# One penalty tile per step, an earlier last batch, and one activation table for exponential and logarithm in a decoder layer

## What is computed

```python
g = sigmoid(x @ Wg + bg)
res = (1 - Z_I) * maximum(1 - Z_I - Z_J, 0) + Z_I * minimum(1 - Z_I + Z_J, 1)   # Z_I = g, Z_J = g transposed
scope = clip(power(s - 2, 1 - g) + 2 - abs_ij, 1e-32, 1.0)
log_pen = log(maximum(res * scope, 1e-32))
scores = q @ k.T / sqrt(16) + log_pen          # 16 heads of 16
x = layernorm(x + softmax(scores) @ v)
x = layernorm(x + cross_attention(x, ctx, mask) @ Wo + bo)
x = layernorm(x + quantised_ffn(x))
```

## Time and profile before

| | us |
|---|---|
| median of 3 runs (lowest, highest) | 772.19 (771.64, 775.09) |
| the profiled execution, its own time | 774.11 |
| its span in the trace | 772.3 |
| PE busy | 659.1 (85%) |
| DVE busy | 591.6 (77%) |
| ACT busy | 489.1 (63%) |
| POOL busy | 327.6 (42%) |

### The profile page before, as it was taken

The page is one execution under the profiler, slowest core; times in us unless marked ns, Lnnn a source line. Parts: engine busy times, 40 slices in busy tenths (PEclk is TensorE's granted clock), DMA queues, the critical chain, the costliest instruction groups (busy, mean ns, idle before and its releaser), DMA issues.

```text
span 772.3 us, 10412 instructions
## 1 busy us (share of the span) xinstructions
PE 659.1 (85%) x3348; PEld 264.2 (34%) x3350; DVE 591.6 (77%) x1299; ACT 489.1 (63%) x809; POOL 327.6 (42%) x417
## 2 busy tenths in 40 slices
PE   6478879999899899998799899998889899984952
PEld 3232224434223243343233343443223235233331
DVE  3988984686899866676997766569986796827986
ACT  4435566556557968654568787554587576773964
POOL 6316766566754414645653135546603110101503
PEclk9778999999999999999999999999999899997977
DMA  2832352320423324313205213342321520000003
GB/s 95 193 93 72 96 135 64 91 60 25 98 60 85 85 44 112 85 44 71 71 24 134 57 52 93 69 109 64 88 65 44 128 59 3 4 3 0 1 0 109
DMA packets 35749, 53.84 MB, mean 70 GB/s; under 512 B 5232, under 2 KB 26736, under 8 KB 35696
## 3 DMA queue, kind: packets, MB, share of 16 engines
q1 hardware_dynamic: 35696, 53.18, 26.5%
HBM read 36.91 MB, written 14.68 MB: 67 GB/s over the span
## 4 chain that ended last, share of the span: by engine, by line
PE 44%; DVE 27%; POOL 11%; ACT 8%; issue 7%; DMA 2%; SPq 0%; POOLq 0%; DVEq 0%; ACTq 0%
PE ps L1583 10%; POOL probs L733 8%; PE ps L1559 8%; PE ps L1536 7%; DVE dist L1026 5%; PE ps L1420 5%; PE ps L1523 5%; DVE mx L1023 4%; ACT probs L918 4%; PE ps L1516 3%; DVE pen_a L1089 2%; DVE pen_a L1085 1%; PE ps L1564 1%; PE ps L1563 1%; DVE pen_a L1093 1%
## 5 line engine op out<-in xcount | busy, mean ns | idle before, releaser
L1536 PE MATMUL ps<-KS,QS 96*128 96x512 bf16 x512 | 201.0, 395 | 36.1 <-DVE mx L1026 13.2
L918 ACT ACTIVATE probs<-ps 128x512 f32<-128x512 f32 x256 | 148.9, 596 | 127.3 <-PE ps L1564 92.3
L733 POOL TENSOR_TENSOR probs<-probs,penT 128x512 f32<-128x512 f32 x128 | 168.5, 1336 | 109.8 <-ACT probs L918 109.8
L1023 DVE TENSOR_REDUCE mx<-ps 128x1 f32<-128x512 f32 x256 | 169.0, 684 | 54.9 <-PE ps L1536 54.3
L1559 PE MATMUL ps<-QS,KS 108*128 108x512 bf16 x512 | 196.6, 386 | 12.9 <-ACT probs L918 9.1
L918 ACT ACTIVATE probs<-ps,mask_col 128x512 f32<-128x512 f32 x256 | 166.6, 689 | 47.1 <-PE ps L1559 45.0
L1026 DVE CUSTOM_DVE_ANT_0 dist<-ps,mask_rest 128x512 bf16<-128x512 f32 x192 | 126.3, 684 | 26.4 <-PE ps L1536 26.1
L1536 PEld LDWEIGHTS ps<-KS,QS 96*128 96x128 bf16 x512 | 50.7, 99 | 186.4 <-DVE mx L1026 64.8
L1559 PEld LDWEIGHTS ps<-QS,KS 108*128 108x128 bf16 x512 | 50.1, 99 | 90.0 <-ACT probs L918 55.1
L1583 PE MATMUL ps<-probs,v_s 128*32 128x512 f32 x512 | 68.2, 604 | 14.3 <-POOL probs L733 14.3
L1583 PE MATMUL ps<-probs,v_c 128*32 128x512 f32 x512 | 69.1, 612 | 0.9 <-ACT probs L918 0.9
(11 more groups left out here) (195 smaller groups left out, 939.5 us busy)
## 6 DMA issues: line engine op xcount, KB each, us to landing
parts_qs<-parts SPq DMA_DIRECT2D x8, 384.0 KB, 2.6
parts_ks<-parts SPq DMA_DIRECT2D x8, 384.0 KB, 2.8
KS<-parts_ks SPq DMA_DIRECT2D x16, 192.0 KB, 3.6
QS<-parts_qs SPq DMA_DIRECT2D x16, 192.0 KB, 4.0
parts_kc<-parts SPq DMA_DIRECT2D x8, 384.0 KB, 2.9
KS<-parts_kc SPq DMA_DIRECT2D x16, 192.0 KB, 3.1
...
```

The lines of the kernel that those rows point to most:

```text
L733: g.tensor_tensor(probs[:, T % NP, :], probs[:, T % NP, :], penT[:, MUL_KT.index(kt), :], ALU.mult)\
L918: s_.activation(probs[:, T % NP, :], ps[:, exp_bank(T), :], ACT.Exp, bias=bias)\
L1023: v.tensor_reduce(mx[:, n % 2, t, j:j + 1], ps[:, MAX_BANKS[(TG * n + i) % AHEAD], :], AX.X, ALU.max)\
L1536: mm(ps[:, MAX_BANKS[(TG * n + i) % AHEAD], :], QS[0:SK, slot, j, t * P:(t + 1) * P], KS[0:SK, slot, j, :], start=True, stop=True).then_in ...
```

## The change

Three things change, all of them in the plan but for one line of ACT.

1. The penalty tiles of batches 1, 2 and 3 are dealt out one to a step, where s02, c00, c01 and c10 had two: batch 1 in s01, s02, s03, s10; batch 2 in s13, c00, c01 and, with seven hand-set slots, c02 and c03; batch 3 in s22, s23, c10, c11. The gate of batch 2 moves from s13 to s12, the fetch of x^T for it from s12 to s10. The logarithm of batch 1 moves from slot 14 of s03 to slot 15 of s10, that of batch 2 from slot 0 of c03 to its slot 15; batch 3's stays.
2. For the last batch the residual, its norm and the two query projections start four to six slots earlier: the residual in slots 1 to 4 of c22 instead of 7 to 10, the norm in 6 to 10 instead of 13 to 15, the first projection in slot 13 of c22 and the second in slot 1 of c23, instead of slots 1 and 5 of c23.
3. ACT loads the table set `natural_log_exp_and_others` at the very start, and the exponential of one column there goes.

```diff
     if what in ("q", "k"):
-        jobs = [(what, *rest, c) for c in range(HC)]
+        jobs = [task] if len(rest) == 3 else [(what, *rest, c) for c in range(HC)]
...
-    add(("s", 0, 2), stacks=[], fetch=[("queries", 0), ("xres", 0)], tasks=[(1, 11, ("k", "s", 1)), (0, 15, ("pens", 1, (1, 2)))])
-    add(("s", 0, 3), at=[(14, ("ln", 1))], fetch=[("mask", 0), ("xres", 1)], tasks=[(0, 13, ("pens", 1, (3,)))])
-    add(("s", 1, 0), fetch=[("masks", 1)], tasks=[(1, 11, ("k", "c", 0)), (8, 14, ("v", "c", 0))])
+    add(("s", 0, 2), stacks=[], fetch=[("queries", 0), ("xres", 0)], tasks=[(1, 11, ("k", "s", 1)), (0, 15, ("pens", 1, (1,)))])
+    add(("s", 0, 3), fetch=[("mask", 0), ("xres", 1)], tasks=[(0, 13, ("pens", 1, (2,)))])
+    add(("s", 1, 0), at=[(15, ("ln", 1))], fetch=[("masks", 1), ("xT", 2)],
+        tasks=[(1, 11, ("k", "c", 0)), (8, 14, ("v", "c", 0)), (0, 11, ("pens", 1, (3,)))])
...
-    add(("s", 1, 2), at=[(1, ("v", "s", 1, 1))], fetch=[("xT", 2)], tasks=[(1, 5, ("residual", 0)), (8, 12, ("ln1", 0))])
-    add(("s", 1, 3), at=[(15, ("mask_col",))], tasks=[(1, 6, ("q", "c", 0)), (7, 8, ("mask", 0)), (3, 14, ("gate", 2))])
-    add(("c", 0, 0), fetch=[("cT", 1)], tasks=[(0, 15, ("pens", 2, (0, 1)))])
-    add(("c", 0, 1), tasks=[(2, 13, ("q", "s", 2)), (0, 15, ("pens", 2, (2, 3)))])
-    add(("c", 0, 2), tasks=[(0, 10, ("k", "s", 2)), (8, 15, ("residual", 1))])
-    add(("c", 0, 3), at=[(0, ("ln", 2))], tasks=[(5, 14, ("v", "s", 2)), (15, 15, ("mask", 1)), (0, 0, ("x1bias", 0)), (2, 13, ("ln1", 1))])
+    add(("s", 1, 2), at=[(1, ("v", "s", 1, 1))], tasks=[(1, 5, ("residual", 0)), (8, 12, ("ln1", 0)), (3, 13, ("gate", 2))])
+    add(("s", 1, 3), at=[(15, ("mask_col",))], tasks=[(1, 6, ("q", "c", 0)), (7, 8, ("mask", 0)), (2, 13, ("pens", 2, (0,)))])
+    last_tile = expand(("pens", 2, (3,)))
+    add(("c", 0, 0), fetch=[("cT", 1)], tasks=[(0, 15, ("pens", 2, (1,)))])
+    add(("c", 0, 1), tasks=[(2, 13, ("q", "s", 2)), (0, 15, ("pens", 2, (2,)))])
+    add(("c", 0, 2), at=[(3 * k, job) for k, job in enumerate(last_tile[:3])],
+        tasks=[(0, 10, ("k", "s", 2)), (8, 15, ("residual", 1))])
+    add(("c", 0, 3), at=[(3 * k, job) for k, job in enumerate(last_tile[3:])] + [(15, ("ln", 2))], tasks=[(5, 14, ("v", "s", 2)), (15, 15, ("mask", 1)), (0, 0, ("x1bias", 0)), (2, 13, ("ln1", 1))])
...
-        add(("s", b, 3), fetch=[("cT", b)] + ([] if more else [("weights", 0)]), tasks=[(0, 9, ("wo", b - 2)), (12, 15, ("ln2", b - 2))])
+        add(("s", b, 3), fetch=[("cT", b)] + ([] if more else [("weights", 0)]), tasks=[(0, 9, ("wo", b - 2)), (12, 15, ("ln2", b - 2))]
+            + ([(0, 13, ("pens", b + 1, (1,)))] if more else []))
...
-            add(("c", b - 1, 0), fetch=[("xres", b)], tasks=[(0, 15, ("pens", b + 1, (1, 2)))])
+            add(("c", b - 1, 0), fetch=[("xres", b)], tasks=[(0, 15, ("pens", b + 1, (2,)))])
...
-            add(("c", b - 1, 2), tasks=[(7, 10, ("residual", b)), (13, 15, ("ln1", b))])
-            add(("c", b - 1, 3), tasks=[(0, 4, ("q", "c", b)), (14, 14, ("x1bias", b))])
+            add(("c", b - 1, 2), tasks=[(1, 4, ("residual", b)), (6, 10, ("ln1", b)), (13, 13, ("q", "c", b, 0))])
+            add(("c", b - 1, 3), tasks=[(1, 1, ("q", "c", b, 1)), (14, 14, ("x1bias", b))])
...
-            act.wait_ge(consts, 1)
-            s_.activation(table_call[:, 0:1], ones_f[:, 0:1], ACT.Exp)
+            s_.preload_act_table_set("natural_log_exp_and_others")
```

## The result

The changed kernel takes 767.5 us, the median of seven runs, beside 773.51 us of the kernel before on the same chip. Six of the seven lie between 763.41 and 768.6 us, and one, at a granted clock of 0.65, took 941.61 us and is left out of the ratio. That is 0.9906, 95% interval 0.9882 to 0.9931. Repeated, it was 0.9930 (0.9905 to 0.9955). So it is faster by 0.7 to 0.9%, some 5 to 7 us, where 20.7 us (to 751.5, range 744 to 763) was forecast: right in sign, a third of the size or less, and outside the range.

The account below looks back on a forecast made before the run. No engine bounds the whole: DVE binds s02, c00, c01 and c10, PE binds s10, s13 and s23. Terms -13.3, -1.5, +0.5, +0.9 - 3.0, +1.5, -2.3, -3.5 sum to -20.7 us: 772.2 to 751.5, range 744 to 763.

Parts of the forecast that it names:

- part 1: One penalty tile per step: s02 -2.5, c00 -4.0, c01 -3.5, c10 -3.3 us, together -13.3.
- The tables' part: Eight table loads go; gains on the path of s10 -1.5, c03 -3.0 and c13 -2.3 us.
- rival 1: Relieved steps meet PE waits DVE hid, give half; s10 gains nothing, s23 loses 3.0; -11.0 us, 761.2; chance 0.20.
- The cost of a tile, (22.5 - 11.4)/15: In s02, DVE's time beyond its maxima over 15 penalty operations: 0.74 us each, 5.2 us per tile of seven.
- c01 by the pattern of c11, 17.8: c01 with one tile was to take 17.8 us like c11, which has the same query projection: -3.5 us.
- s10 (-1.5): Table loads give 2.6 us less about 1.1; the added tile is hidden under PE's 21.6 us.
- s12 and s13 (+0.5): Batch 2's gate moves to s12 (+3.0 us); s13 loses it and takes a tile (-2.5 us).
- c02 and c03 (-2.1): Shared tile 3 of batch 2 costs +0.9 us; table loads and half clock gone from c03 give -3.0.
- c13 (-2.3), s23 (+1.5): c13 loses two table loads, 2.6 us less 0.3; s23 takes a tile, 0 to +5.2 us.
- rival 3: Each of six table loads on the path also costs a drain, 1.28 us: 7.7 us more, 743.8; chance 0.03.
- The last batch (-3.5): c22, c23 and c30: PE's 2.4 us query-stack wait and a third of 3 us of clock go; range 0 to -7.
- Rival 2: mT is late at slot 8 of c23 and the clock halves behind it: 3.5 us lost, 755.0; chance 0.12.

Follow-up runs that it names:

- the tables alone: Kernel before with only the first exponential replaced by one table-set load: 0.9873, and 0.9914 on another chip.
- short products: Changed kernel with POOL's multiplications of probabilities by penalties cut from 512 to 64 columns: 732.83 us in one execution.
- the product a slot later: Context product of multiplied tiles one slot later on PE, in kernels with table load and mT first: 0.9834, repeated 0.9857, with old tile places; 0.9800 with moved.
- the second trace: Changed kernel run again with nothing altered, against the kernel before: 0.9930.
- mT first: Kernel before with table load and last batch moved, shift row mT sent between c30's key and query loads, tiles in old places: 0.9901.

## Why the prediction was wrong, point by point

**The step that failed.** It is part 1: -13.3 us for four relieved steps, and -10.4 for the moved tiles as a whole. Alone they gave nothing (1.0002, 0.9986 to 1.0018). By PE's starts and against the tables alone the four relieved steps give 5.5 us, and s12, c03, s23, s10 and s11, less s13, take some 6.3, for which 2.9 was booked. Two things were wrong in it, the next bound and the price of a tile. The tables' part came out as forecast (6.2 of 6.8 us).

**The reading of the four steps as bound by DVE: half right.** "s02 falls to DVE 17.3 and PE 19.2, say 20.0" took PE's busy time as the next bound. The row that spoke against it stood in the earlier trace rows: POOL was busy for 18.20 us in s02, in bursts of four multiplications with PE's context product fixed three slots behind. With six of seven penalty operations gone altogether s02 takes 21.38 us; with short products 19.00. What was named was a wait that DVE hid, but only in rival 1, at a chance of 0.20, and there without its owner. With the product a slot later s02 gives 2.1 us by PE's starts, near the 2.5 of the forecast, and c00 3.0 of 4.0, but c01 gives 1.1 of 3.5 and c10 1.4 of 3.3: together 7.6 of 13.3. So the step that priced the next bound lacked POOL, and with POOL out of the way the mechanism is right in s02 and c00, and close to half of the sum is still missing. Why c01 and c10 give so little was not tested; in c10 DVE is busy for 20.08 of 20.11 us with its one tile.

**The cost of a tile, (22.5 - 11.4)/15.** 5.2 us is what a tile occupies, not what it costs. Part of it is time beside POOL: the operation of line 1098 takes 409 to 426 ns with POOL idle and 1104 to 1516 with POOL at work. Taking out six of its seven operations gave about 0.9 us per tile. That the operation is dearer beside POOL was read. What was not read is that its place beside POOL's bursts sets its length, so that moving it changes the work: s02 gave back 1.6 us of DVE's operations and not 5.2 (2.7 in the second trace), s10, s13 and s23 took 7.5, 8.2 and 6.9, and DVE's busy time grew by 10.9 us in all. DVE's 22.50 of 22.50 us was no measure of its work.

**c01 by the pattern of c11, 17.8.** c11's window was short because the step ahead was bound by DVE, whose maxima then run late and catch up: by PE's starts c11 takes 18.8 and 18.7 us in the two kernels. Of the windows' -2.8 and -2.7 for c01 and c10, PE's starts leave 1.9 and 1.3; the rest came back in c02 (+1.7) and c11 (+1.0). c00's -3.4 is -1.3 by PE's starts, while s13, level by its window, is -1.0.

**s10 (-1.5).** Came as +0.1. The table loads alone gave 0.6, and the tile, priced at nothing under PE's 21.6 us, took it back, with 0.6 more in s11. PE's waits for POOL were the missing cover: with the later product s10 and s11 take the tile at 0.0.

**s12 and s13 (+0.5).** s12 was right: +3.0 (+2.5 in the second trace). s13's -2.5 was wrong: by PE's starts it gave 1.0, and by its window nothing, with the later product too (23.51). Taking the tile's operations out gives 0.6 us there by PE's starts, so the gate's leaving gave some 1.6, less than the 2.3 to 2.7 that it costs s12. Which of s13's other waits takes its place is open.

**c02 and c03 (-2.1).** The loads gave 3.6 here, more than the 3.0 of the forecast, since the whole half-clock stretch behind them (269 to 273 us) went with them. Tile 3 costs 2.2 in c03, which has four of its operations, and by PE's starts nothing in c02; 0.9 was booked for the pair: it stands among the norm of batch 1 and the value projection, in a step where DVE is busy for 18.18 of 19.21 us with it and 15.2 of 17.0 without.

**c13 (-2.3), s23 (+1.5).** Came as -2.0 and +1.4. Here the load is 2 x 1.28 us on the path, less what came late next. The Trainium skill, page "ScalarE: Activation LUTs", section "What ACT_TABLE_LOAD costs", puts every switch at 2.66 us with its drain, which makes an estimate of 5.3 us for the two. The trace does not agree: the measured gain is 2.0 us, and the next instruction starts 0.02 us behind each load in the earlier trace rows. In this kernel the switch costs its load alone, and rival 3 is out.

**The last batch (-3.5).** Rival 2 happened, in the place it named: PE waits 1.6 us for mT at slot 8 of c23 and the clock halves. What was wrong is the comparison of "4 slots against 1.4 us": mT was late by 1.6 us because it waits behind a store's landing and three loads. And the half clock of c30, for which 1 of the 3.5 us was booked, went away in kernels that leave this part out. Alone this part is worth nothing (0.9995). With mT first, c22 to c30 take 51.4 us beside 52.5 with the tables alone, but two half-clock stretches elsewhere (363 and 520 us) eat that: spans of 763.3 and 763.1, ratios of 0.9901 and 0.9914.

**Chances.** Rival 1 (-11.0 us) and rival 2 together give 3.5 less, -7.5, near the 5 to 7 us that were measured. Each was priced alone against an otherwise full forecast, and the cautious end of the range should have been made from both. That their sum comes so near is partly luck: s12 with s13 and c02 with c03 lost 5 us against the forecast that neither rival names, while the windows of the relieved steps gave more than rival 1 has.
